# The normalised x tile moves from VectorE to ScalarE at the head of a step, its statistics one tile ahead, and the attention bias is loaded early

## The chip, the cores and the metric

The kernel runs on one core of a Trainium2 chip. The metric is the device time of one execution in microseconds (us). Three executions of the kernel before took 1130.46, 1130.94 and 1133.43 us, with a median of 1130.94 us. TensorE (PE) does the matrix products, VectorE (DVE) and ScalarE (ACT) the work on vectors and the copies out of PSUM, GpSimd (POOL) small work in SBUF, and SyncE (SP) issues nearly all DMAs.

## The reference

One gated cross-attention layer of a Flamingo model, all in f32. x has the shape (4, 2048, 512), the context (4, 77, 384); there are 16 heads of 64, and the feed-forward part is one matrix that is picked out of eight.

```python
def _layernorm(x, axis=-1, eps=1e-05):
    m = jnp.mean(x, axis=axis, keepdims=True)
    v = jnp.var(x, axis=axis, keepdims=True)
    return (x - m) / jnp.sqrt(v + eps)
...
    q = split_heads(x @ Wq)
    k = split_heads(context @ Wk)
    v = split_heads(context @ Wv)
    sim = jnp.einsum('bhid,bhjd->bhij', q, k) * SCALE
    attn = jax.nn.softmax(sim, axis=-1)
    out = jnp.einsum('bhij,bhjd->bhid', attn, v)
    out = out.transpose(0, 2, 1, 3).reshape(b, sq, HEADS * DIM_HEAD)
    return out @ Wo + bo
...
    gumbel = -jnp.log(-jnp.log(u))
    idx = jnp.argmax(jax.nn.log_softmax(logits) + gumbel)
    out = jnp.einsum('btd,de->bte', x, W[idx]) + b[idx]
...
    x = x + jnp.tanh(g_xattn[0]) * _L0_xattn_ref(_layernorm(x), ctx_768, Wq, Wk, Wv, Wo, bo)
    x = x + jnp.tanh(g_ffn[0]) * _L0_ffn_ref(_layernorm(x), W, b, logits, u)
```

## The kernel before, in words

**Folding.** Before the tiles are touched, the query and key weights are folded with the context into one matrix of 512 x (16 x 77) for each of the four batches (`a_split`), and the value and output weights with it into a second one (`vw`, `vw_side`). After that a tile of 128 rows of x needs only this: normalise x (`xn`), multiply by `a_split` (the scores), take the softmax over 77 keys for each head, multiply by `vw` (this is the attention with Wo and bo in it), add to x, normalise again, multiply by the picked feed-forward matrix, add to x.

**Two halves of every number.** Every operand of the large products is f32 split into two f16 halves, a high and a low one, and three products are added up. So each operand passes over ACT (the high half: `x_high`, `probs_high`, `group_high`) and then over DVE (the low half, `low` at L412: `x_low`, `probs_low`, `group_low`), and is then turned (transposed) by a DMA from SP.

**Tiles and steps.** There are 64 tiles. A step `(o, m)` works on tile number 8o+m and on its neighbours; 66 steps run, the first 6 and the last ones unrolled, the others as 7 rounds of a loop of 8 steps (`steps`, L324 to L332). `tile(o, m, lag)` is the tile `lag` steps ahead (o1, m1: the next tile; o2, m2: two tiles back). Every engine has its own `step` with its own hand-written order, and semaphores tie them together.

**The order on each engine in one step of the kernel before**, for tile m:
- PE: the three banks of scores of tile m (`scores`, L1443, 36 products), two products of the feed-forward pair, the attention of tile m-1 (`attention`, L1461), further products of the pair (two in an even step, one in an odd one). The seven products of a pair of tiles are spread over two steps. All pass the helper at L1288. The scores wait for `xT_turned`, the attention for `pT_turned`.
- DVE (L1210): additions of products (`added`, L1191), the moments of x of tile m+1 (L953), the aggregation for tile m-2 (L1147), the largest score of bank 0 (`maxima`, L1111 and L1113), the aggregation for tile m+1 (L957), a low half of a pair group, normalisation of tile m-2 (L1158), bank 1, **the normalisation of x of tile m+1 (`x_normalized`, L964)**, bank 2, additions, **`x_low`**, the softmax factors (L1120, L1122), the low halves of the probabilities, and the sum for the attention of tile m-1 (L1140, L1143).
- ACT (L879): a high half of a pair group (L840), the exponentials of banks 0 and 1 (L817, one instruction a head), **`x_high` (L731) of tile m+1**, another group, the exponentials of bank 2, the high halves of the probabilities (L832, L834, L905).
- POOL (L670): variance to 1/sqrt for tile m-2 (L676, L678) and for tile m+1 (`x_scale`, L601, L603), sums for the pair groups (L692 to L699), the bias (L703).
- SP (L487): in an even step it stores two finished tiles (L497), then loads two tiles of x (L459, after the stores have landed), turns group 2, turns x of tile m+1 (`turn_x`, L444), turns group 3; in an odd step group 0, x, group 1. Last in a step it turns the probabilities (L551).

**Where things lie.** `xn` lies in the room of the high and low probabilities (`ps_words`), so it can be written only when the probabilities of the tile before have been turned. There is one place for the turned x (`xT`), so it is turned only when the scores of tile m are done.

**The prologue.** SP loads context, value weights, two small inputs, output weights, key weights, the picked matrix, query weights, and then the attention bias `bo` (L436) and the first tile. DVE takes the largest value of the output weights, then waits for `bo` (L986), and only behind this come the parts for the value weights, which end in the scale of the folded values. The list VISITS (L346) orders the folding; some units are split on POOL by way of a staging copy (`staged`, `key_staged`). After it DVE works out five small scales (L1090 to L1103). The feed-forward matrix is brought again, four sums of its quarters are made on POOL (`weights_summed`), and its seven operands are split by ACT in step 1 (`weights_high`) and DVE in step 2 (`weights_low`).

## Time and profile before

| what | value |
|---|---|
| median of three executions | 1130.94 us |
| profiled execution | 1130.8 us |
| its span in the trace | 1129.0 us |
| PE busy | 1054.2 us (93%) |
| DVE busy | 884.6 us (78%) |
| ACT busy | 688.2 us (61%) |
| POOL busy | 350.3 us (31%) |
| DMA engines busy, over the whole | 55.5% |

The span runs from the first to the last instruction; 1.8 us of the profiled execution lie around it. A busy share says how long an engine had an instruction in it; it does not say which engine sets the time. In the rows below `[1.04 <-DMA work<-work]` means that the engine had been idle for 1.04 us before this group, and that a DMA from `work` to `work` (a turn) ended the wait. The core's granted TensorE clock was 0.982 of full speed over the span.

### The profile page before, as it was taken

Reading aid. Unit: us, or ns where it says so; the run is one execution under the profiler, and the core shown is the slowest. Engines: PE = TensorE matmul, PEld = TensorE weight load, DVE = VectorE, ACT = ScalarE, POOL = GpSimd, SP = SyncE. Lnnn points to the kernel's source line nnn. Section 1 sums busy time; section 2 is a strip of 40 time slices with the busy share of each in tenths; the row PEclk is TensorE's granted clock in tenths of the full one; section 3 lists DMA queues with packets and bytes.
Section 4 is the critical chain, followed back from the end, with each engine's and each line's share of the span. In section 5 each row is a group of like instructions: output and inputs, shape, how many; then the busy total and the mean of one; then the engine's idle time right before and its main releaser. Section 6 shows DMA issues by size and latency. Waiting matters only on the chain.

```text
span 1129.0 us, 21540 instructions
## 1 busy us (share of the span) xinstructions
PE 1054.2 (93%) x6109; PEld 592.2 (52%) x6109; DVE 884.6 (78%) x1853; ACT 688.2 (61%) x2645; POOL 350.3 (31%) x504
## 2 busy tenths in 40 slices
PE   7778789999999999899999999999989999899997
PEld 5433435555554555555555555555545555455555
DVE  2757778878888888788878887888878888888883
ACT  3257666566656666566666666666657665666670
POOL 0167233223332233322233332333223333223311
PEclk9799989999999999999999999999999999999999
DMA  8131246666665555666566555556665655655563
GB/s 314 39 57 57 61 94 117 127 121 127 131 118 112 112 120 126 127 131 130 119 124 126 125 117 106 114 128 132 135 121 118 135 123 108 121 116 121 126 118 103
DMA packets 381682, 134.33 MB, mean 119 GB/s; under 512 B 360160, under 2 KB 361236, under 8 KB 381588
## 3 DMA queue, kind: packets, MB, share of 16 engines
q1 hardware_dynamic: 381524, 133.43, 55.5%
q14 instruction: 78, 0.64, 0.2%
q8 instruction: 16, 0.26, 0.1%
q0 software_dynamic: 64, 0.00, 0.0%
HBM read 27.21 MB, written 16.78 MB: 39 GB/s over the span
## 4 chain that ended last, share of the span: by engine, by line
DVE 23%; DMA 17%; issue 17%; ACT 16%; PE 15%; SPq 10%; POOL 1%; DVEq 1%; ACTq 0%
ACT work L817 12%; DMA work<-work 11%; PE banks L1288 10%; DVE work L412 6%; SPq L551 6%; DMA out<-work 4%; DVE work L1122 3%; DVE stats L1111 2%; DVE work L1140 2%; DVE stats L953 2%; DVE stats L1143 2%; ACT work L731 2%; SPq L463 2%; DVE work L1191 1%; DVE cst L1120 1%
## 5 line engine op out<-in xcount | busy, mean ns | idle before, releaser
L817 ACT ACTIVATE work<-banks,red,cst 128x77 f32<-128x77 f32 x1024 | 409.8, 423 | 199.8 <-DVE red L1113 198.8
L1288 PE MATMUL banks<-fold_area,work 128*128 128x462 f16 (+1 forms) x2304 | 417.9, 341 | 40.9 <-DMA work<-work 38.9
L1288 PE MATMUL banks<-vw_area,work 128*128 128x512 f16 x1701 | 378.9, 381 | 5.2 <-issue 5.2
L1288 PEld LDWEIGHTS banks<-fold_area,work 128*128 128x128 f16 x2304 | 223.7, 98 | 227.6 <-DMA work<-work 36.6
L412 DVE SCALAR_TENSOR_TENSOR work<-work 128x256 f16<-128x256 f32 (+3 forms) x444 | 241.9, 586 | 119.8 <-ACT work L731 70.7
L1288 PEld LDWEIGHTS banks<-vw_area,work 128*128 128x128 f16 x1701 | 166.4, 98 | 194.2 <-issue 7.5
L817 ACT ACTIVATION_READ_ACCUMULATOR work<-banks,red,cst 128x1 f32 x1024 | 217.0, 212 | 0.0
L676 POOL TENSOR_TENSOR stats<-stats,cst 128x1 f32<-128x1 f32 x64 | 12.1, 189 | 653.9 <-DVE stats L1147 653.9
L840 ACT ACTIVATE work<-work 128x512 f16<-128x512 f32 x124 | 72.5, 585 | 146.0 <-DMA work<-work 128.8
L1288 PE MATMUL banks<-work 128*128 128x256 f16 x1260 | 157.2, 273 | 0.0
L1288 PEld LDWEIGHTS banks<-work 128*128 128x128 f16 x1260 | 123.0, 98 | 30.1
L1191 DVE SCALAR_TENSOR_TENSOR work<-banks,cst,work 128x256 f32<-128x256 f32 x210 | 97.0, 482 | 28.8 <-issue 18.1
L1111 DVE TENSOR_REDUCE stats<-banks 128x6 f32<-128x462 f32 (+1 forms) x192 | 111.1, 579 | 10.2 <-PE banks L1288 7.6
L1122 DVE TENSOR_TENSOR work<-work,cst 128x924 f32<-128x924 f32 (+1 forms) x128 | 102.4, 800 | 4.4
L832 ACT ACTIVATE work<-work 128x768 f16<-128x768 f32 (+1 forms) x128 | 80.6, 630 | 22.3 <-DVE work L1122 22.3
L703 POOL TENSOR_TENSOR work<-work 128x512 f32<-128x512 f32 x64 | 81.2, 1269 | 7.1 <-DVE work L1158 6.1
L1113 DVE TENSOR_SCALAR red<-stats,cst 128x6 f32<-128x6 f32 (+1 forms) x192 | 69.8, 364 | 6.8
L1140 DVE SCALAR_TENSOR_TENSOR work<-banks,cst,work 128x512 f32<-128x512 f32 x64 | 47.7, 746 | 4.8 <-PE banks L1490 4.7
L1143 DVE BATCH_NORM_STATS2 stats<-work 128x6 f32<-128x512 f32 x64 | 44.5, 695 | 2.2
L731 ACT ACTIVATE work<-work 128x512 f16<-128x512 f32 x64 | 41.7, 652 | 4.9 <-DVE work L964 4.9
L953 DVE BATCH_NORM_STATS2 stats<-work 128x6 f32<-128x512 f32 x64 | 43.7, 683 | 0.1
L603 POOL TENSOR_TENSOR stats<-stats,cst 128x1 f32<-128x1 f32 x64 | 41.5, 648 | 5.0
(122 smaller groups left out, 751.5 us busy)
## 6 DMA issues: line engine op xcount, KB each, us to landing
work<-in_x SPq DMA_DIRECT2D x64, 256.0 KB, 2.8
out<-work SPq DMA_DIRECT2D x64, 256.0 KB, 2.2
work<-work SPq DMA_TRANSPOSE x258, 3.2
fold_area<-in_L_xattn_Wo SPq DMA_DIRECT2D x4, 512.0 KB, 10.1
work<-in_L_ffn_W SPq DMA_DIRECT2D x2, 1024.0 KB, 7.1
fold_area<-in_L_xattn_Wq SPq DMA_DIRECT2D x2, 1024.0 KB, 13.0
fold_area<-in_L_xattn_Wk SPq DMA_DIRECT2D x2, 768.0 KB, 12.2
fold_area<-in_L_xattn_Wv SPq DMA_DIRECT2D x2, 384.0 KB, 7.4
```

The lines of the kernel that those rows point to most:

```text
L412: return nc.vector.scalar_tensor_tensor(out=lo, in0=value, scalar=scale, in1=hi, op0=ALU.mult, op1=ALU.subtract)
L551: sp.dma_start_transpose(turned[:, start:, :], ps[:, start * P:]).then_inc(pT_turned, 16)
L703: nc.gpsimd.tensor_tensor(xr[:, m2, :], xr[:, m2, :], bias, ALU.add).then_inc(x2b_ready, 1)
L817: nc.scalar.activation(probs[:, h * J:(h + 1) * J], s_bank(m, k)[:, (h - h0) * J:(h - h0 + 1) * J], ACT.Exp, bias=nmx[:, h:h + 1], scale=e ...
L832: nc.scalar.activation(by_core(ps[:, h0 * CORE:h1 * CORE]), values[:, :, 0:CORE], ACT.Copy, scale=2.0 ** PROB_BITS).then_inc(p_hi, 1)
L840: nc.scalar.activation(group_stage(g)[:, 0, :], value, ACT.Copy, scale=2.0 ** XN_BITS).then_inc(x2_hi, 1)
L1111: nc.vector.reduce_max(mx[:, h0:h1], by_head(s_bank(m, k)), AX.X).then_inc(mx_ready, 1)
L1113: nc.vector.tensor_scalar(nmx[:, h0:h1], mx[:, h0:h1], nexp_scale, None, ALU.mult).then_inc(nmx_ready, 1)
L1122: nc.vector.tensor_tensor(values, values, factors.unsqueeze(2).to_broadcast([P, h1 - h0, J]), ALU.mult).then_inc(p_ready, 1)
L1140: nc.vector.scalar_tensor_tensor(out=xr[:, m, :], in0=o_ps, scalar=o_scale, in1=xr[:, m, :], op0=ALU.mult, op1=ALU.add).then_inc(x2_ready, 1)
L1191: nc.vector.scalar_tensor_tensor(out=half, in0=part, scalar=f_scale, in1=half, op0=ALU.mult, op1=ALU.add).then_inc(f_added, 1)
L1288: mm = nc.tensor.matmul(ps, lhs(l), rhs(r), start=first and n == 0, stop=last and n == 2, skip_group_check=onto)
```

## The change

`xn` is made by ACT instead of DVE, as x times rstd plus (-mean times rstd), for which POOL makes two more small values. ACT does it first in a step, followed at once by `x_high`. Its place is now the second half of `xs` and the first 256 words of `probs`; the probabilities are rotated so that these words belong to the four heads of bank 2, and the exponentials of bank 2 wait for `x_low`. The moments and the scale of x are made for tile m+2 at the end of step m. DVE's order within a step, SP's order in an even step and POOL's order change with it. In the prologue `bo` is loaded before the output weights, the last two staged key units are no longer staged, the small scales are made at KEY 20, the first tile is normalised earlier, and the work on the feed-forward weights is split over two steps. The idle products at the first attention go from 14 to 22.

```diff
         def xn_place(o, m):
-            if is_tile(o, m, 0, 1, 2):
-                return room_a if m == 2 else room_b
-            return ps_words[:, 0:D]
+            return room_b if is_tile(o, m, 0, 1) else xn_late      # xn_late = at(folds - HD, D)
         def key_staged(v):
-            return v % HP in STAGED_KEYS
+            return v < UNITS - HP and v % HP in STAGED_KEYS
+        def probs_of(h0, h1):
+            first = (h0 * J - BANKS[2][0] * J) % HJ
+            return probs[:, first:first + (h1 - h0) * J]
# SP
+            sp.dma_start(room_b, bo...).then_inc(bo_loaded, 16)        # ahead of wo
-            sp.dma_start(room_b, bo...).then_inc(bo_loaded, 16)        # behind wq
-                    for lag in (2, 3):
-                        ... load_x(ol, ml)                             # ahead of turn_group(2)
+                    for lag in (2, 3):
+                        ... load_x(ol, ml)                             # behind turn_group(2)
# POOL
             def x_scale(q1, b1):
                 pool.wait_ge(x_var, nth(q1, b1) + 1)
                 nc.gpsimd.tensor_tensor(ve1, mv1[:, 1:2], eps, ALU.add).then_inc(ve1_ready, 1)
-                pool.wait_ge(ve1_ready, nth(q1, b1) + 1)
+                nc.gpsimd.tensor_tensor(nmean1, mv1[:, 0:1], neg_one, ALU.mult).then_inc(ve1_ready, 1)
+                pool.wait_ge(ve1_ready, nth(q1, b1, 2) + 2)
                 nc.gpsimd.tensor_tensor(rstd1, ve1, neg_half, ALU.pow).then_inc(x_rstd, 1)
+                pool.wait_ge(x_rstd, nth(q1, b1, 2) + 1)
+                nc.gpsimd.tensor_tensor(nm1, nmean1, rstd1, ALU.mult).then_inc(x_rstd, 1)
# POOL, step: x_scale of tile m+2 last, behind the pair sums and the bias (it was of tile m+1, early)
# ACT
+            def x_normalized(o1, m1):
+                act.wait_ge(x_rstd, nth(o1, m1, 2) + 2)
+                if not is_tile(o1, m1, 0, 1):
+                    act.wait_ge(xT_turned, nth(o1, m1, 16))
+                    act.wait_ge(p_lo, nth(o1, m1, 4) - 4)
+                nc.scalar.activation(xn_place(o1, m1), xr[:, m1, :], ACT.Identity, bias=nm1, scale=rstd1).then_inc(xn_ready, 1)
 # exponentials
+                if k == 2 and valid(o1):
+                    act.wait_ge(x_lo, nth(o1, m1) + 1)
 # step
+                if valid(o1):
+                    x_normalized(o1, m1)
+                    x_high(o1, m1)
                 if grouped:
                     group_high_of(*pair, 2 if m % 2 == 0 else 0)
                 if valid(o):
                     exponentials(o, m, 0)
                     exponentials(o, m, 1)
-                if valid(o1) and not is_tile(o, m, 0):
-                    x_high(o1, m1)
+                if is_tile(o, m, 0):
+                    weights_high(AS_LOADED)          # places 0, 1, 6
                 if is_tile(o, m, 1):
-                    weights_high()
+                    weights_high(AS_SUMMED)          # places 4, 3, 2, 5
# DVE, the order of a step after the change
+                added 6 / added 2, 3;  maxima 0;  group_low 2 or 0;  x2_variance;  maxima 1;  x2_normalized
+                maxima 2;  x_low(m+1);  [weights_low in steps 1 and 2];  added 0, 1 / 4, 5;  softmax 0
+                group_low 3 or 1;  x_moments(m+2);  softmax 1;  x_variance(m+2);  probs_low 0, 1;  attention_sum(m-1)
# PE
-                    keep_running(14)
+                    keep_running(22)
```

## Rows read from the trace of the kernel before

**Rows 1.** The page, busy time of the engines
```profile
PE 1054.2 (93%) x6109; PEld 592.2 (52%) x6109; DVE 884.6 (78%) x1853; ACT 688.2 (61%) x2645; POOL 350.3 (31%) x504
```

**Rows 2.** Waits of PE: us in total, times, longest us
```profile
PE banks L1288 <- DMA work<-work: 38.9, 28, 5.3
```

**Rows 3.** Timeline of PE: start us, us, what; first instructions of scores
```profile
188.12 6.42 PE L1288 MATMUL banks<-fold_area,work 128*128 128x462 f16 x36
...
361.78 6.42 PE L1288 MATMUL banks<-fold_area,work 128*128 128x462 f16 x36
391.40 6.42 PE L1288 MATMUL banks<-fold_area,work 128*128 128x462 f16 x36
...
560.66 6.42 PE L1288 MATMUL banks<-fold_area,work 128*128 128x462 f16 x36
576.35 6.43 PE L1288 MATMUL banks<-fold_area,work 128*128 128x462 f16 x36 [1.04 <-DMA work<-work]
594.32 8.11 PE L1288 MATMUL banks<-fold_area,work 128*128 128x462 f16 x36 [2.65 <-DMA work<-work]
...
1088.92 6.42 PE L1288 MATMUL banks<-fold_area,work 128*128 128x462 f16 x36
```

**Rows 4.** Timeline of ACT, DVE and SP, one step
```profile
566.33 0.42 ACT L817 ACTIVATE work<-banks,red,cst 128x77 f32<-128x77 f32 x1 [4.47 <-DVE red L1113]
571.05 0.66 ACT L731 ACTIVATE work<-work 128x512 f16<-128x512 f32 x1
...
560.62 1.65 DVE L412 SCALAR_TENSOR_TENSOR work<-work 128x768 f16<-128x768 f32 x4 [0.55 <-ACT work L834]
568.90 0.47 DVE L1111 TENSOR_REDUCE stats<-banks 128x4 f32<-128x308 f32 x1
571.75 1.22 DVE L412 SCALAR_TENSOR_TENSOR work<-work 128x512 f16<-128x512 f32 x1 [1.30 <-ACT work L731]
...
573.19 1.23 SPq L449 DMA_TRANSPOSE work<-work  x1
```

**Rows 5.** Busy time in a stretch: PE, PEld, DVE, ACT, POOL, PEclk, DMA
```profile
396.00:528.00 132.00, 127.45 (x739) 71.58 (x737) 108.06 (x233) 85.40 (x350) 39.94 (x59) 1.00 0.60 127
```

**Rows 6.** Groups of DVE and ACT between 188.12 and 1088.92 us, shapes apart
```profile
L964 DVE TENSOR_SCALAR work<-work,stats 128x512 f32<-128x512 f32 x58 | 32.0, 552 | 0.7 <-DMA work<-work 0.7
L412 DVE SCALAR_TENSOR_TENSOR work<-work 128x512 f16<-128x512 f32 x145 | 112.4, 775 | 62.1 <-ACT work L731 62.1
L817 ACT ACTIVATE work<-banks,red,cst 128x77 f32<-128x77 f32 x928 | 371.4, 422 | 180.6 <-DVE red L1113 179.7
```

**Rows 7.** The page, groups of POOL
```profile
L603 POOL TENSOR_TENSOR stats<-stats,cst 128x1 f32<-128x1 f32 x64 | 41.5, 648 | 5.0
```

**Rows 8.** Timeline of DVE behind the loop's end
```profile
581.43 0.48 DVE L1191 SCALAR_TENSOR_TENSOR work<-banks,cst,work 128x256 f32<-128x256 f32 x1 [2.99 <-issue]
```

**Rows 9.** The page, DMA issues: KB each, us from issue to landing
```profile
work<-in_x SPq DMA_DIRECT2D x64, 256.0 KB, 2.8
```

**Rows 10.** Timeline of SP, an even step
```profile
584.38 0.97 SPq L459 DMA_DIRECT2D work<-in_x  x2
```

**Rows 11.** Timeline of DVE and PE, prologue
```profile
31.48 0.69 DVE L987 TENSOR_REDUCE cst<-work 128x1 f32<-128x512 f32 x1 [12.00 <-DMA work<-in_L_xattn_bo]
...
25.20 0.27 PE L1294 MATMUL banks<-work,red 128*128 128x128 f32 x1
36.42 0.48 PE L1294 MATMUL banks<-work,red 128*128 128x128 f32 x1 [10.95 <-DVE red L938]
```

**Rows 12.** Timeline of DVE and PE, later prologue
```profile
81.30 0.55 DVE L964 TENSOR_SCALAR work<-work,stats 128x512 f32<-128x512 f32 x1 [2.91 <-POOL stats L603]
...
111.77 12.68 PE L1288 MATMUL banks<-fold_area,work 128*128 128x462 f16 x72 [1.93 <-POOL fold_area L636]
```

**Rows 13.** Timeline of PE, first steps
```profile
139.69 6.43 PE L1288 MATMUL banks<-fold_area,work 128*128 128x462 f16 x36 [0.67 <-DMA work<-work]
157.65 8.25 PE L1288 MATMUL banks<-fold_area,work 128*128 128x462 f16 x36 [5.27 <-DMA work<-work]
```

More of the change, by code:

```diff
@@ L117, in flamingo_layer @@
         c.at = RING * D
-        xs = c.take(D).bitcast(F16).rearrange("p (s n) -> p s n", s=2)
         xT = c.take(D)
@@ L151, in flamingo_layer @@
         free = x2T_at + KT * D
-        v_stage = [at(free, 2 * D).rearrange("p (e n) -> p e n", e=2), at(x2T_at, 2 * D).rearrange("p (e n) -> p e n", e=2)]
+        v_stage = [at(start, 2 * D).rearrange("p (e n) -> p e n", e=2) for start in (x2T_at, free)]
         side_stage = [at(start, B * HEADS * REST).rearrange("p (b n) -> p b n", b=B) for start in (x2T_at + 2 * D, free)]
@@ L373, in key_staged @@
         def key_staged(v):
-            return v % HP in STAGED_KEYS
+            return v < UNITS - HP and v % HP in STAGED_KEYS
         def key_staged_before(v):
-            return v // HP * len(STAGED_KEYS) + sum(h < v % HP for h in STAGED_KEYS)
+            return sum(key_staged(n) for n in range(v))
         def highs_after(n):
@@ L507, in step @@
                         turn_group(2)
+                    for lag in (2, 3):
+                        ol, ml = tile(o, m, lag)
+                        if valid(ol):
+                            load_x(ol, ml)
                     if valid(o1) and not is_tile(o, m, 0):
@@ L670, in step @@
             def step(o, m):
-                o1, m1 = tile(o, m, 1)
+                on, mn = tile(o, m, 2)
                 o2, m2 = tile(o, m, -2)
@@ L874, in weights_high @@
                 act.wait_ge(scale_f_ready, 1)
-                act.wait_ge(wf_summed, 4)
-                for i, part in enumerate((b11, b21, t2, b12, t1, t4, b22)):
+                act.wait_ge(wf_again, 16)
+                for i in places:
+                    if i == 4:
+                        act.wait_ge(wf_summed, 4)
+                    part = (b11, b21, t2, b12, t1, t4, b22)[i]
                     nc.scalar.activation(wf_split[:, i, 0], part, ACT.Copy, scale=scale_f).then_inc(wf_hi, 1)
@@ L893, in step @@
                     exponentials(o, m, 1)
-                if valid(o1) and not is_tile(o, m, 0):
-                    x_high(o1, m1)
                 if grouped:
@@ L1212, in step @@
                 o1, m1 = tile(o, m, 1)
+                on, mn = tile(o, m, 2)
                 op, mp = tile(o, m, -1)
@@ L1219, in step @@
                 multiplied = valid(begun[0]) and paired(*begun)
-                ahead = valid(o1) and not is_tile(o, m, 0)
-                if valid(o2):
-                    dve.wait_ge(x2_stats, nth(o2, m2) + 1)
                 if even and valid(ended[0]) and paired(*ended):
@@ L1246, in step @@
                 if valid(o):
-                    maxima(o, m, 1)
-                if ahead:
-                    x_normalized(o1, m1)
-                if valid(o):
                     maxima(o, m, 2)
+                if valid(o1):
+                    x_low(o1, m1)
+                if is_tile(o, m, 1):
+                    weights_low(AS_LOADED, 0)
+                if is_tile(o, m, 2):
+                    weights_low(AS_SUMMED, len(AS_LOADED))
                 if multiplied:
@@ L1254, in step @@
                     added(*begun, 1 if even else 5)
-                if ahead:
-                    x_low(o1, m1)
-                if grouped and even:
-                    group_low_of(*pair, 3)
                 if valid(o):
                     softmax(o, m, 0)
-                    softmax(o, m, 1)
-                if grouped and not even:
-                    group_low_of(*pair, 1)
+                if grouped:
+                    group_low_of(*pair, 3 if even else 1)
                 if not even and is_tile(*pair, 2 * PAIRS):
                     lone_low(2 * PAIRS + 1)
+                if valid(on):
+                    x_moments(on, mn)
+                if valid(on):
+                    dve.wait_ge(x_stats, nth(on, mn) + 1)
+                if valid(o):
+                    softmax(o, m, 1)
+                if valid(on):
+                    x_variance()
                 if valid(o):
```

111 lines of the change are left out of this document (52 added, 59 removed).

## The prediction

> **What bounds the kernel now.** I read the page's busy shares first. PE is busy for 93% of the span, DVE for 78%, ACT for 61% [rows 1]. PE is the candidate, and only a cut in what PE waits for can save much. Second, PE's waits: the scores wait for a turned x 28 times, 38.9 us in all [rows 2]. Third, PE's timeline, read from the start of one tile's scores to the next. Where nothing waits, two tiles (an even and an odd step) take PE 29.62 us, 361.78 to 391.40, 14.81 each [rows 3]. From tile 5 (188.12) to tile 63 (1088.92) lie 29 pairs in 900.8 us. At 29.62 us they would take 859.0, so **41.8 us** are lost to waits and what follows them: after 2.65 us of waiting the scores of 594.32 took 8.11 us instead of 6.42 [rows 3]. The trace as a whole gives a granted clock of 0.982, so a part of the loss is TensorE at its lower level of 1.2 GHz behind such a pause.
>
> Fourth, one step on the other engines, to see why x is late. The scores start at 560.66. DVE reads the last bank at 568.90, but x's high half starts on ACT only at 571.05, because it stands in ACT's queue behind twelve exponentials that begin at 566.33. DVE has waited 1.30 us for it, writes the low half from 571.75, SP turns it from 573.19, and PE starts at 576.35, 3.16 us after that issue and 1.04 us late [rows 3, 4]. DVE pays this wait in nearly every step: 62.1 us over 58 steps, 1.07 each, and 0.55 us for each normalisation [rows 6]. Meanwhile ACT sits idle before the exponentials, 4.47 us here and 180.6 us in 58 steps, 3.1 each [rows 4, 6].
>
> Last, the prologue. DVE stands 12.00 us at L987 for the attention bias. PE spreads a first maximum at 25.20 and the second only at 36.42, 10.95 us idle [rows 11].
>
> **Part 1, x at the head of ACT's step.** ACT gets one more instruction of 128x512. The nearest rows are the high half, 0.66 us on ACT, and the same normalisation on DVE, 0.55 [rows 4, 6]; this one reads two values per partition, so I put it between 0.55 and 1.0 us and take 0.7. Together with the high half that is 1.4 us, set where ACT idles for 3.1 us on the average [rows 6]. Cost on the path: nothing. If that cover is gone, it is 1.4 us a step behind which all exponentials queue, then the softmax on DVE.
>
> The rule of the Trainium skill that speaks against this is in "ScalarE: Activation LUTs", Rules for kernel authors: add and multiply belong on VectorE, which is the faster per element. Its section What ACT_TABLE_LOAD costs gives 186 + 0.833 N ns and some 93 ns for each pointer operand, by which an estimate for this instruction is 0.80 us. The rows agree that DVE is the faster (0.55 against 0.66), and by the page alone 64 tiles would lose 16 us; the rule looks at one instruction, and the idle time of ACT makes it cheap here, so it changes nothing in the sum.
>
> DVE loses the 0.55 us and the wait of 1.07, 1.6 us a step, of 108.06 us busy in 132 (some 13.0 a step at 124 us for eight) [rows 5, 6]. Left are some 12.4 us of work, against 14.81 of PE. Two waits are new. The new place makes ACT wait for the low halves of the step before; these end about 562.3, just where ACT's idle stretch of 4.47 us begins [rows 4], so this costs nothing unless DVE falls behind. The exponentials of bank 2 wait for `x_low`; behind them queue ACT's high halves and, on DVE, the second softmax. `x_low` follows bank 2's maximum: 568.90 + 0.47, its negation (put at 0.47 too, as it is smaller), and 0.78 for the low half [rows 4, 6] make 570.6. ACT is through banks 0 and 1 at 571.05, and has a group to do yet. Hidden by 0.4 us and the group; without cover ACT waits out the difference.
>
> The turn of x then starts near 570.7 instead of 573.19, 2.5 us earlier, and with the same 3.16 us it lands at 573.9, where PE comes free at 575.3 (576.35 - 1.04) [rows 3, 4]. So the usual wait goes with 1.4 us to spare, and DVE starts its next step earlier besides. What is late next? The turned probabilities. They leave at the end of DVE's step and are used only behind the next scores (6.4 us) and two products; I expect no wait.
>
> **Part 2, the statistics one tile ahead.** POOL gets two more operations on 128x1, at most 0.65 us each [rows 7], and is busy for 31% [rows 1]. The chain now has from the end of one step to the head of the next; three dependent operations make under 2 us (3 x 0.65), while DVE still writes the low halves (1.65 us and its wait of 0.55 [rows 4]). Nothing on the path. The tile loaded in an even step is now read by DVE in the same step. SP issues the loads at 584.38 today, 3.0 us behind DVE's first addition at 581.43; moved behind a turn of 1.23 us they go out near 585.5 and land 2.8 us later, at 588.3 and 588.8 [rows 4, 8 to 10]. DVE reaches these moments behind twelve exponentials, 4.72 us (566.33 to 571.05), that begin some 2 us into its step, and behind the first softmax; that makes 589 or later. Nothing, with little to spare. For its price without them, see the last rival.
>
> **Part 3, the loop's end.** At each of the 7 ends DVE stands still for about 3 us with no one to wait for (2.99 in the row) [rows 8]; the wait and slow scores at 594.32 follow from it. The change does not touch this. The Trainium skill, "Runtime: NRT & Kernel Launch", Instruction fetch mechanics, says that a taken branch out of the fetched window stops the sequencer until its page is there, which agrees with the row. DVE would be 3 us late, and so is x: undisturbed DVE is to issue the turn 8 to 10 us behind the start of scores, with 3 us more 11 to 13, and it lands 3.16 later, at 14.2 to 16.2 against 14.81. I take 3 us as left over in all seven, nearer to the lower end because DVE also starts its step earlier; bounds are 0 and 7 x (2.65 + 1.69) = 30 us [rows 3]. So the steady part gives 41.8 - 3 = **38.8 us**.
>
> **Part 4, the bias early.** Its load goes 3 places up; 256 KB ahead of the output weights delays these by an issue and under 1 us of transfer, and those 12.00 us of waiting nearly vanish. But then DVE meets PE's first spread at 25.20 [rows 11]. Behind it stand a power of two, two parts and the largest, put at 1.9 us together (the row of 128x512 at L987 took 0.69, and they are about as much each or less), so the second spread falls at 27.1 instead of 36.42: **9.3 us**, if loads behind it are in time (the bias itself, last but one, landed at 31.48, and its place is taken by the query weights). Bounds 3 and 12; the nearest row is the 10.95 of PE's idleness.
>
> **Part 5, the later prologue.** The first tile's normalisation leaves DVE, which waited 2.91 us there for POOL. The last staged units leave POOL, for which PE waits 1.93 us before the first scores [rows 12], and come to DVE with two low halves, while the normalisation of tile 1 goes and the small scales move there. I count 2 us from the first and 0.7 from the second: **2.7 us**, bounds 0 and 5.
>
> **Part 6, the first steps.** From the first scores (111.77) to those of tile 2 (139.69) 27.92 us pass [rows 12, 13]. After the change the scores of tile 1 cannot follow at once, as its low half comes behind bank 2 of tile 0: 6.3 (half of 12.68) + 0.47 + 0.47 + 0.78 + 3.16 = 11.2 us after the first. They take 6.4 to 8.1 us, the attention 6.3 (139.69 to 157.65 less the wait of 5.27 and the scores of 6.43), and the 22 idle products, for which no row stands, 2 to 3: 26 to 29 us. I take no change. Then tile 3 waited 5.27 us and its scores took 8.25 instead of 6.43 [rows 13]; this came of DVE and ACT doing seven operands in a row ahead of x. 7.1 us less, of which I give 0.7 back, as DVE has some 13 us of work and latency in a step while PE has 12.7 (6.43 + 6.3) without pair products: **6.4 us**, bounds 2 and 9.
>
> **Sum.** 38.8 + 9.3 + 2.7 + 6.4 = 57.2 us, on a span of 1129.0 that becomes 1071.8; with the 1.8 us around it 1073.6 for an execution. The profiled one (1130.8) stands 0.1 us off the median of 1130.94, so I predict **1074 us**. The tail behind 1088.92 is bound by PE, which no edit shortens there. Highest of all gains: 41.8 + 12 + 5 + 9 = 68, so 1063; lowest: 12 + 3 + 0 + 2 = 17, so 1114.
>
> **Rivals.** (A) *The loop's end stays on the path.* For it speaks that DVE's 3 us come in one piece and that it has 2.4 us a step to make good; against it, that the turn leaves 2.5 us earlier. With 2.65 us left at each of seven ends, and three or four of them slowing the scores by 1.69, 24 us stay instead of 3: 1074 + 21 = 1095 us. (B) *The prologue is bound by its loads or by DVE behind the bias.* DVE had 108.06 of 132 us in the loop and is as dense in the prologue; then the 9.3 us shrink to 3 and part 5 to 0: 1074 + 9 = 1083. (C) *It isn't earlier*: ACT reaches its head late, because its group high halves wait for DMAs, and x's low half still comes at the old time. Then only prologue and first steps gain: 1131 - 18 = 1113. Against it: ACT's 3.1 us of idleness a step. (D) *Slower: the moments wait for their tile.* In every even step DVE, in order, stands at the moments until load and turn have landed, and all behind it (second softmax, low halves, the attention's sum) waits. PE feels it once it has eaten DVE's spare time, 2 x 2.4 us a pair, and with 2.1 us more a pair (41.8 + 18.4 us of gain over 29 pairs) all is lost: from 6.9 us of waiting on the kernel is slower than before. At 8 us it is 1074 + 29 x (8 - 4.8) = 1167. Against it: 2.8 us from issue to landing [rows 9].
>
> **Chances.** Forecast (1064 to 1083) 0.60, A 0.14, B 0.14, C 0.06, D 0.03, no change for any reason 0.03. Range 1063 to 1096 leaves out C, D and the rest. 0.3% is what a measurement can tell here. Faster 0.94, same 0.03, slower 0.03.
>
> **What would show it.** After the change PE's waits for a turn are under 8 us in all, pairs start 29.6 to 30 us apart, also over a loop's end; the turn of x is issued 8 to 10 us behind the start of scores (573.19 - 560.66 = 12.5 before); the second spread is near 27 us; the first scores near 100. Wrong would be: ACT idle ahead of its new instruction for a DMA or POOL; DVE waiting for a load at the moments; scores still at 8 us.

## The result, and the profile after

Four executions of the changed kernel took 1075.98 to 1078.66 us, median 1077.25; of the kernel before, beside it, 1129.03 to 1133.43. The ratio is 0.9525, interval 0.9503 to 0.9548: **53.5 us less, 4.75%**. Predicted were 1074 us and 1063 to 1096. The profiled execution took 1076.78 us, with a span of 1075.0 against 1129.0.

The busy line of the page [rows 1]: PE is the same 1045 to 1054 us busy, now 97% of the span. DVE has lost 35 us, ACT has gained 55 and POOL 81, and none of that is on the path.

```profile
PE 1045.0 (97%) x6117; PEld 593.9 (55%) x6117; DVE 849.8 (79%) x1791; ACT 743.4 (69%) x2709; POOL 431.3 (40%) x629
```

PE's waits [rows 2], in total, times, longest: before, PE waited 28 times for a turned x. Now it waits for one twice (5.8 us, ahead of the scores, `fold_area`) and twice for turned probabilities (4.6 us, ahead of the attention, `vw_area`). All four stand in the first steps; the last wait of the kernel, 3.50 us, is in the tail. The scores of tile 5 begin at 173.36, those of tile 63 at 1032.34, and in between PE waits for nothing.

```profile
PE banks L1308 <- DMA work<-work: 10.3, 4, 4.6
```

PE's timeline (start, duration, what, idle before) for the rows of [rows 3, 11 to 13]: the second spread at 27.35 (36.42 before), the first scores at 96.56 (111.77), the first steps with their four waits, two steady scores a pair (29.62 us) apart, and the tail.

```profile
27.35 0.32 PE L1314 MATMUL banks<-work,red 128*128 128x128 f32 x1 [1.71 <-DVE red L967]
...
96.56 8.10 PE L1308 MATMUL banks<-fold_area,work 128*128 128x462 f16 x36 [2.08 <-issue]
109.26 9.16 PE L1308 MATMUL banks<-fold_area,work 128*128 128x462 f16 x36 [4.59 <-DMA work<-work]
...
140.76 6.43 PE L1308 MATMUL banks<-fold_area,work 128*128 128x462 f16 x36 [1.16 <-DMA work<-work]
151.02 6.00 PE L1308 MATMUL banks<-vw_area,work 128*128 128x512 f16 x27 [3.83 <-DMA work<-work]
...
165.77 6.00 PE L1308 MATMUL banks<-vw_area,work 128*128 128x512 f16 x27 [0.76 <-DMA work<-work]
...
380.70 6.42 PE L1308 MATMUL banks<-fold_area,work 128*128 128x462 f16 x36
...
410.32 6.42 PE L1308 MATMUL banks<-fold_area,work 128*128 128x462 f16 x36
...
1066.57 5.10 PE L1556 MATMUL banks<-work 128*128 128x256 f16 x30 [3.50 <-DMA work<-work]
```

From these rows the 54.0 us of span divide, beside the terms of the prediction:

| stretch | before | after | difference | predicted |
|---|---|---|---|---|
| start to the first scores | 111.77 | 96.56 | -15.2 | -12.0 |
| first scores to those of tile 5 | 76.35 | 76.80 | +0.45 | -6.4 |
| tile 5 to tile 63 | 900.8 | 858.98 | -41.8 | -38.8 |
| tile 63 to the end | 40.1 | 42.7 | +2.6 | 0 |

One steady step [rows 4, 5], timeline of DVE, POOL, ACT and SP, tile scores starting at 558.42:

```profile
557.22 0.81 POOL L608 TENSOR_TENSOR stats<-stats,cst 128x1 f32<-128x1 f32 x1 [4.83 <-DVE stats L986]
558.42 6.42 PE L1308 MATMUL banks<-fold_area,work 128*128 128x462 f16 x36
559.42 0.81 ACT L743 ACTIVATE work<-work,stats 128x512 f32<-128x512 f32 x1 [1.49 <-POOL stats L613]
560.27 0.63 ACT L750 ACTIVATE work<-work 128x512 f16<-128x512 f32 x1
564.87 0.48 DVE L1131 TENSOR_REDUCE stats<-banks 128x4 f32<-128x308 f32 x1 [0.21 <-PE banks L1308]
565.39 0.23 DVE L1133 TENSOR_SCALAR red<-stats,cst 128x4 f32<-128x4 f32 x1
565.52 0.69 DVE L418 SCALAR_TENSOR_TENSOR work<-work 128x512 f16<-128x512 f32 x1
566.45 1.23 SPq L455 DMA_TRANSPOSE work<-work  x1
```

x's high half is ready at 560.90, before the last bank of scores exists. The low half follows the last maximum at once, and the turn of x goes out 8.0 us behind the start of scores (12.5 before). From there it is 6.4 us to the next scores, for a turn that took 3.16 before. DVE, which used to wait for ACT, now waits for PE (91.1 us before its maxima, 1.57 a step). That is what a step bound by PE looks like. Busy time over eight steps (columns as in [rows 5]) gives DVE 98.10 / 8 = 12.3 us a step, and PE all 118.50:

```profile
388.00:506.50 118.50, 118.50 (x690) 67.09 (x689) 98.10 (x213) 85.89 (x329) 49.16 (x73) 1.00 0.61 129
```

### The profile page after: what moved, and what is told of

It reads as the page before. It is cut to its first block, busy times and chain, and to the rows that moved or that the text cites. A ratio compares the mean times of both kernels' runs of the same rounds, so it can differ in the third digit from the quotient of the medians.

```text
span 1075.0 us, 21893 instructions
## 1 busy us (share of the span) xinstructions
PE 1045.0 (97%) x6117; PEld 593.9 (55%) x6117; DVE 849.8 (79%) x1791; ACT 743.4 (69%) x2709; POOL 431.3 (40%) x629
## 4 chain that ended last, share of the span: by engine, by line
PE 90%; DVE 3%; DMA 2%; ACT 2%; POOL 1%; issue 1%; SPq 0%; ACTq 0%
PE banks L1308 82%; PE banks L1510 2%; DMA work<-work 1%; PE banks L1338 1%; PE banks L1347 1%; PE banks L1556 1%; PE banks L1419 1%; ACT work L840 1%; PE banks L1411 1%; DVE vw_area L1042 1%; DMA fold_area<-in_L_xattn_Wv 1%; PE banks L1400 1%; DVE work L418 0%; DVE fold_area L1050 0%; ACT vw_area L793 0%
## 5 line engine op out<-in xcount | busy, mean ns | idle before, releaser
L840 ACT ACTIVATION_READ_ACCUMULATOR work<-banks,red,cst 128x1 f32 x1024 | 224.6, 219 | 0.0
L687 POOL TENSOR_TENSOR stats<-stats,cst 128x1 f32<-128x1 f32 x64 | 12.1, 190 | 294.4 <-DVE stats L1167 294.4
L608 POOL TENSOR_TENSOR stats<-stats,cst 128x1 f32<-128x1 f32 x64 | 50.7, 792 | 186.2 <-DVE stats L986 186.2
L743 ACT ACTIVATE work<-work,stats 128x512 f32<-128x512 f32 x64 | 52.1, 814 | 95.1 <-POOL stats L613 79.4
L1142 DVE TENSOR_TENSOR work<-work,cst 128x924 f32<-128x924 f32 (+1 forms) x128 | 112.7, 880 | 4.4
L1211 DVE SCALAR_TENSOR_TENSOR work<-banks,cst,work 128x256 f32<-128x256 f32 x210 | 94.7, 475 | 21.8 <-issue 18.4
L709 POOL TENSOR_TENSOR work<-work 128x512 f32<-128x512 f32 x64 | 94.5, 1477 | 40.9 <-DVE work L1178 36.8
L863 ACT ACTIVATE work<-work 128x512 f16<-128x512 f32 x124 | 71.8, 579 | 21.8 <-DVE work L1178 17.1
L1133 DVE TENSOR_SCALAR red<-stats,cst 128x6 f32<-128x6 f32 (+1 forms) x192 | 60.1, 313 | 6.8
```

What stands on the lines that cost most here:

```text
L608: nc.gpsimd.tensor_tensor(ve1, mv1[:, 1:2], eps, ALU.add).then_inc(ve1_ready, 1)
L709: nc.gpsimd.tensor_tensor(xr[:, m2, :], xr[:, m2, :], bias, ALU.add).then_inc(x2b_ready, 1)
L743: nc.scalar.activation(xn_place(o1, m1), xr[:, m1, :], ACT.Identity, bias=nm1, scale=rstd1).then_inc(xn_ready, 1)
L840: nc.scalar.activation(probs_of(h, h + 1), s_bank(m, k)[:, (h - h0) * J:(h - h0 + 1) * J], ACT.Exp, bias=nmx[:, h:h + 1], scale=exp_scale, ...
L863: nc.scalar.activation(group_stage(g)[:, 0, :], value, ACT.Copy, scale=2.0 ** XN_BITS).then_inc(x2_hi, 1)
L1133: nc.vector.tensor_scalar(nmx[:, h0:h1], mx[:, h0:h1], nexp_scale, None, ALU.mult).then_inc(nmx_ready, 1)
```

## The experiments

Each kernel ran beside the kernel before on the same chip. Its median there was 1130.8 to 1132.5, so ratios are compared where kernels measured in different groups meet.

### The bias alone

The kernel before, with only this:

```diff
+ sp.dma_start(room_b, bo...).then_inc(bo_loaded, 16)   # ahead of wo
- sp.dma_start(room_b, bo...).then_inc(bo_loaded, 16)   # behind wq
```

> The kernel before with one edit: the attention bias is loaded ahead of the output weights. Theory (as in part 4 of the prediction, with what the changed kernel showed): the second spread on PE falls to about 27.3 us from 36.4, and everything behind keeps the shift, so 9 to 12 us are gained, a time of 1119 to 1122; of the 15.2 us by which the first scores came earlier in the changed kernel the rest (3 to 6 us) belongs to the other edits of the prologue. Rival: the loads or DVE bind behind it and under 5 us are gained (1126 or more).

1121.41 us (1119.65 to 1122.63), ratio 0.9905 [0.9889, 0.9922]: 10.1 us less. PE's timeline:

```profile
26.63 0.32 PE L1294 MATMUL banks<-work,red 128*128 128x128 f32 x1 [1.72 <-DVE red L938]
...
99.53 12.68 PE L1288 MATMUL banks<-fold_area,work 128*128 128x462 f16 x72 [1.93 <-POOL fold_area L636]
```

The second spread moved 9.8 us, the first scores 12.2 (99.53). So one DMA, issued ahead of nine others instead of behind them (the loads of four weights), is worth a fifth of the whole change. The other edits of the prologue brought 3 us by this trace (99.53 to 96.56), but in kernels with the changed prologue the first scores begin anywhere from 93.1 to 97.3, so 2 to 6 us is all that can be said.

### The place in ACT's queue

The changed kernel, with ACT's two instructions behind the exponentials instead of ahead of them. Engine, room and statistics are as changed.

```diff
-                if valid(o1):
-                    x_normalized(o1, m1); x_high(o1, m1)
...
                     exponentials(o, m, 0)
                     exponentials(o, m, 1)
+                if valid(o1):
+                    x_normalized(o1, m1); x_high(o1, m1)
```

> The changed kernel, but ACT normalises x and makes its high half behind the exponentials of banks 0 and 1, where the high half stood before, and not first in a step; all else stays. Theory A (the place in ACT's queue is what freed PE): DVE again waits at the low half, 1 us or more a step, the turn leaves some 2 us later, and PE waits for x again at least at the ends of the loop: 1085 to 1110. Theory B (what freed PE is the work taken off DVE and the statistics a tile ahead, the place in the queue is not needed): DVE's spare time takes the wait and the time stays within 3 us of the changed kernel's 1077.

1147.61 us (1145.41 to 1148.38), ratio 1.0142 [1.0125, 1.0159]. **The change turns from 54 us faster into 16 slower.** Timeline of ACT and DVE, and DVE's waits:

```profile
568.63 0.85 ACT L743 ACTIVATE work<-work,stats 128x512 f32<-128x512 f32 x1
569.51 0.63 ACT L750 ACTIVATE work<-work 128x512 f16<-128x512 f32 x1
570.17 0.86 DVE L418 SCALAR_TENSOR_TENSOR work<-work 128x512 f16<-128x512 f32 x1 [3.31 <-ACT work L750]
571.13 0.42 ACT L840 ACTIVATE work<-banks,red,cst 128x77 f32<-128x77 f32 x1 [0.47 <-DVE work L418]
```
```profile
DVE work L418 <- ACT work L750: 190.5, 63, 8.4
```

ACT is not short of time; its order makes DVE wait 3.0 us a step. I had expected 1085 to 1110. I had counted the lateness of x and left out that the exponentials of bank 2 wait in turn for the low half (the row of 571.13): the two engines wait for each other, one after the other, inside one step. That second wait exists only because the changed kernel keeps `xn` in the room of bank 2's probabilities, so the 70 us or so between the two kernels are the place in the queue and this room together.

### The engine alone

The kernel before, with the normalisation on ACT just ahead of `x_high` in its old place, and the two small values on POOL for it.

```diff
 # ACT, x_high
+                act.wait_ge(x_rstd, nth(o1, m1, 2) + 2)
+                nc.scalar.activation(xn_place(o1, m1), xr[:, m1, :], ACT.Identity, bias=nm1, scale=rstd1)...
 # DVE, step
-                    x_normalized(o1, m1)
```

> The kernel before, but x is normalised by ACT directly in front of its high half, in the old place in ACT's queue and in the old room; POOL makes the two small values; statistics and order as before. Theory A (it is the place in the queue): x is later by ACT's 0.8 us less what DVE's lost 0.55 us gives back, so 0 to 20 us slower, 1131 to 1151. Theory B (it is the offload): DVE's 0.55 us a step come off the path, up to 30 us faster, 1100 to 1115.

1163.65 us (1163.04 to 1164.32), ratio 1.0282 [1.0265, 1.0299]: 32 us slower. DVE's wait for the high half went from 1.07 us a step [rows 6] to 2.5:

```profile
DVE work L412 <- ACT work L741: 160.0, 63, 4.5
```

So taking 0.55 us off DVE is a loss where the 0.8 us that replace it stand on the path. Again I had the sign and too small a size (1131 to 1151 expected).

### The place without the engine

The changed kernel again, for reference, and beside it one in which DVE normalises, as the last thing in the step before; ACT then begins its step with the high half.

```diff
 # DVE, step, last
+                if valid(on):
+                    x_normalized(on, mn)
 # ACT, step, first
-                    x_normalized(o1, m1)          # kept for tile 1
                     x_high(o1, m1)
```

> The changed kernel itself, once more, as the measure for the other runs of this group on the same chip: both theories expect 1075 to 1079 us.

> The changed kernel, but x of tile m+2 is normalised by DVE, last in step m behind the sum for the attention, in the new place; ACT makes only the high half first in a step. Theory A (what matters is that x's high half stands ahead of the exponentials, not which engine normalises): DVE has some 12.3 us of work in 14.81 and takes 0.55 more, so PE still waits for nothing in the loop: within 3 us of the changed kernel. Theory B (the offload from DVE is needed too): DVE's 0.55 us a step and its late end show on PE, 10 to 32 us slower than the changed kernel.

The changed kernel: 1074.52 us (1073.24 to 1076.34), ratio 0.9501 [0.9479, 0.9524]. DVE normalising: 1072.53 (1070.65 to 1076.82), ratio 0.9491 [0.9463, 0.9519]. No difference can be told. In its timeline the high half comes 3.2 us behind the start of scores (554.84), against 1.9 in the changed kernel; the turn of x goes out 8.7 us behind it, and PE waits for it in no steady step:

```profile
557.43 0.53 DVE L994 TENSOR_SCALAR work<-work,stats 128x512 f32<-128x512 f32 x1
558.08 0.63 ACT L750 ACTIVATE work<-work 128x512 f16<-128x512 f32 x1 [2.69 <-DVE work L994]
```

**In the steady part the change buys the place at the head of ACT's step, with its statistics ready; who normalises does not matter.** No run has that place without the statistics a tile ahead, the new room and DVE's new order, so what each of these adds was not measured.

### How much time DVE has to spare

The changed kernel with two, and with four, more `bn_stats` of 128x512 a step on DVE behind the moments, their results unused.

```diff
                     x_moments(on, mn)
+                    for i in range(2):            # and 4
+                        nc.vector.bn_stats(stats[:, 56:62], xr[:, mn, :])...
```

> The changed kernel with two more DVE instructions in every step, moments of the same x tile into unused words, behind the real ones: 1.4 us more of DVE work a step, nothing else. Theory A (DVE has 12.3 us of work, its spare time is 2.5 us a step less the stop of 3 us at a loop's end): 13.7 us still fit in 14.81, PE may wait at the loop's ends for 0 to 2 us each; 1075 to 1090. Theory B (DVE is all but the bound): 1.4 x 58 = up to 80 us slower, 1110 or more.

> The same with four more DVE instructions a step, 2.7 us. Theory A: 12.3 + 2.7 + 0.4 (the stop spread over 8 steps) = 15.4 against 14.81, so DVE becomes the bound and the kernel takes about 0.6 x 58 = 35 us more, 1095 to 1130. Theory B (DVE is all but the bound already): twice the loss of the kernel with two, 1140 to 1235.

With two: 1077.7 us (1074.75 to 1080.06), ratio 0.9531 [0.9508, 0.9554], 3 us above the reference, with overlapping intervals. Over eight steps PE is never idle and DVE is busy for 106.73 of 118.50 us, 90%:

```profile
388.00:506.50 118.50, 118.50 (x689) 66.97 (x688) 106.73 (x229) 85.24 (x329) 49.34 (x73) 1.00 0.61 129
```

With four: 1165.64 (1164.2 to 1167.06), ratio 1.0297 [1.0274, 1.032]. Busy time over 240 us of its loop, then waits of ACT and PE in the whole kernel:

```profile
260.00:500.00 240.00, 221.46 (x1256) 122.05 (x1254) 221.29 (x448) 157.47 (x611) 86.86 (x131) 0.99 0.58 121
```
```profile
ACT work L855 <- DVE work L1142: 220.5, 63, 5.2
...
PE banks L1312 <- DMA work<-work: 54.6, 36, 6.5
```

Eight steps take 131.0 us here (387.13 to 518.17), 16.38 each; DVE is busy for 92% of that, 15.1 us. The work alone, 12.26 + 4 x 0.69 = 15.0, is only 0.2 us over PE's 14.81, yet the step grew by 1.57. DVE's other 1.2 us a step (9.8 us in these eight) are 3.0 us of standing still at the loop's end, 3.1 of waits for the exponentials, the group's high half and POOL, and 3.7 of gaps for which the profile names no wait. The stop and the gaps stand in the changed kernel too, where DVE had time over. I had expected 1095 to 1130 from the work and the stop alone.

How much DVE has to spare lies between the two runs. With two added instructions it still waits for the scores, 4.4 us in eight steps (13.5 in the changed kernel), so its spare time was over 1.4 us a step. With four, 2.8 us, it is gone and PE waits. Why the step then grows by 1.57 us, more than the sum of the work says, is explained only in part.

### The first steps: bias x gate

The first steps were the one term with the wrong sign. Timeline of ACT, DVE and SP in step 2 of the changed kernel:

```profile
134.67 0.72 ACT L912 ACTIVATE work<-work,cst 128x512 f32<-128x512 f32 x1 [5.28 <-DMA work<-in_L_ffn_b]
135.29 0.80 ACT L743 ACTIVATE work<-work,stats 128x512 f32<-128x512 f32 x1
136.13 0.63 ACT L750 ACTIVATE work<-work 128x512 f16<-128x512 f32 x1
136.79 0.69 DVE L418 SCALAR_TENSOR_TENSOR work<-work 128x512 f16<-128x512 f32 x1 [2.67 <-ACT work L750]
137.66 1.24 SPq L455 DMA_TRANSPOSE work<-work  x1
```

An instruction that is run once, the feed-forward bias times its gate, waits for its DMA at the very head of ACT's queue. It stood there before as well. In the trace of the kernel before, ACT waits 3.67 us for the same load in step 2, but DVE is at its seven low halves in a row until 148.2 and has the maximum of bank 1 only at 150.1:

```profile
147.52 0.72 ACT L886 ACTIVATE work<-work,cst 128x512 f32<-128x512 f32 x1 [3.67 <-DMA work<-in_L_ffn_b]
```
```profile
143.56 4.69 DVE L1207 SCALAR_TENSOR_TENSOR work<-work,red 128x512 f16<-128x512 f32 x7
...
149.29 0.79 DVE L1113 TENSOR_SCALAR red<-stats,cst 128x6 f32<-128x6 f32 x1
```

The six exponentials of bank 1 cannot start before that, and x's high half, behind them, came at 152.86. By these rows the load delayed it by some 0.4 us at most. The change splits the seven operands over two steps and puts x ahead of the exponentials; this cover is gone, and the load alone holds x. The experiment moves the instruction:

```diff
-                if is_tile(o, m, 2):
-                    act.wait_ge(bias_loaded, 16); act.wait_ge(gate_ready, 1)
-                    nc.scalar.activation(bias, bias, ACT.Copy, scale=gates[:, 1:2])...
 ...                 # x_normalized, x_high, group, exponentials 0 and 1
+                if is_tile(o, m, 2):
+                    ... the same three lines
```

> The changed kernel with one edit: the multiplication of the feed-forward bias by its gate, which ACT does first in step 2 and for which it waits 5.28 us for a load, comes behind the exponentials of banks 0 and 1 of that step. Theory A (this wait at the head of ACT's step 2 took away the gain of the first steps that was forecast at 6.4 us): x of tile 3 and the softmax of tile 2 come some 4 us earlier, PE's waits of 1.16 and 3.83 us at 140.8 and 151.0 go, and the time falls by 3 to 6 us to 1071 to 1074. Theory B (the first steps are bound by DVE and the slow TensorE clock instead): within 1.5 us of the changed kernel.

1071.94 us (1068.13 to 1073.06), ratio 0.9465 [0.9442, 0.9489]; and once more on another chip, as the control of what follows:

> The control of the two kernels below, the same kernel as the one with bias x gate moved behind the exponentials of banks 0 and 1 in step 2 (no other difference from the changed kernel). It gave 1071.94 us beside 1131.54 for the kernel before. Expected here: 1068 to 1074 us, ratio 0.945 to 0.949. If it comes at 1075 or above, the gain that I put down to the move of bias x gate was scatter of the prologue.

1071.62 us (1069.92 to 1074.96), ratio 0.9474 [0.9448, 0.9501]. PE's wait ahead of tile 3's scores is gone, the one behind them has shrunk from 3.83 to 1.90:

```profile
97.34 6.42 PE L1308 MATMUL banks<-fold_area,work 128*128 128x462 f16 x36 [2.08 <-issue]
108.34 8.71 PE L1308 MATMUL banks<-fold_area,work 128*128 128x462 f16 x36 [4.58 <-DMA work<-work]
...
138.06 6.42 PE L1308 MATMUL banks<-fold_area,work 128*128 128x462 f16 x36
146.38 6.00 PE L1308 MATMUL banks<-vw_area,work 128*128 128x512 f16 x27 [1.90 <-DMA work<-work]
```

From the first scores to tile 5's it is 71.3 us here and 75.3 in the reference run of the changed kernel, both with the first scores at full clock: 4.0 us, in the expected 3 to 6. In the first run of this kernel it is 74.7 us, since its first scores ran at the lower clock (9.28 us). Read from the scores of tile 2 to those of tile 5, which leaves that scatter out, it is 46.4 and 47.3 us in the two traces of the changed kernel and 43.1 in both with the move: 3.3 to 4.2 us. The intervals of the whole times overlap with the reference, so the gain rests on the traces.

### The first steps: the wait for tile 1, and the loads

Two more on top of that. First idle products in PE's wait for the turned x of tile 1; then the loads of tiles 2 and 3 in the prologue as well, with fewer idle products at the first attention.

```diff
 # PE, step, ahead of scores
+                if is_tile(o, m, 1):
+                    all_folded(); keep_running(38)
```
```diff
 # SP, prologue, behind the load of tile 1; left out in step 0
+            sp.dma_start(xr[:, 2, :], x[2, 0:P, :]).then_inc(x_loaded[2], 16)
+            sp.dma_start(xr[:, 3, :], x[3, 0:P, :]).then_inc(x_loaded[3], 16)
 # PE, attention
-                    keep_running(22)
+                    keep_running(8)
```

> As the control, and TensorE fills its wait for the turned x of tile 1 with idle products (38 of the small ones that it already uses elsewhere in the prologue), ahead of the scores of tile 1; nothing of the computation changes. In the changed kernel the scores of tile 1 took 9.16 us after 4.59 us idle, and those of later tiles 6.42. Theory A (TensorE runs slower for a while after it stood idle): the scores of tile 1 take about 6.4 us, and what follows comes 1.7 to 2.7 us earlier: 2 to 2.7 us below the control. Theory B (the next thing that TensorE waits for, the turned probabilities of tile 0, lands when it lands, whatever TensorE does before): the scores are shorter and the wait behind them longer by as much, no difference beyond 0.7 us.

> As the kernel with the filled wait, and x of tiles 2 and 3 is loaded in the prologue right behind tile 1's, where before both were loaded in step 0, and the idle products ahead of the first attention are cut from 22 to 8. In the changed kernel VectorE's moments of tile 2 wait 2.4 us for that load in step 0. Theory A (this wait stands ahead of the first attention's low halves): 1.5 to 2.4 us below the kernel with the filled wait. Theory B: what VectorE waits for next (the exponentials by ScalarE) takes the place of it, no difference beyond 0.7 us; or the two loads push the weights that the folding waits for, and it is slower by up to 2 us.

The filled wait: 1067.78 us (1066.81 to 1069.56), ratio 0.9446 [0.9422, 0.9469], 3.8 below the control. The loads early: **1062.8 us** (1062.59 to 1067.16), ratio **0.9411** [0.9385, 0.9437], a further 5.0 by the medians, with intervals that overlap a little. PE's timelines, of the filled wait first:

```profile
102.85 4.31 PE L1321 MATMUL banks<-work 128*128 128x128 f32 x38
107.59 6.43 PE L1308 MATMUL banks<-fold_area,work 128*128 128x462 f16 x36 [0.43 <-DMA work<-work]
113.86 2.56 PE L1321 MATMUL banks<-work 128*128 128x128 f32 x22
116.26 5.99 PE L1308 MATMUL banks<-vw_area,work 128*128 128x512 f16 x27
```
```profile
94.90 6.42 PE L1310 MATMUL banks<-fold_area,work 128*128 128x462 f16 x36 [2.08 <-issue]
...
105.89 6.43 PE L1310 MATMUL banks<-fold_area,work 128*128 128x462 f16 x36 [0.43 <-DMA work<-work]
112.15 1.04 PE L1323 MATMUL banks<-work 128*128 128x128 f32 x8
113.03 5.99 PE L1310 MATMUL banks<-vw_area,work 128*128 128x512 f16 x27
...
1054.03 3.44 PE L1558 MATMUL banks<-work 128*128 128x256 f16 x30 [3.48 <-DMA work<-work]
```

The granted clock from 105 to 118 us was 0.74 in the control and 1.00 with the wait filled: the 4.58 us of standing still had sent PE to its lower level (1.2 of 2.4 GHz) for a part of the next scores, 8.71 instead of 6.43 us. From first scores to tile 5's it is 71.3, then 68.0, then 65.9 us. Of the first 3.3 us, 2.3 lie between the scores of tile 1 and of tile 2, as expected (2 to 2.7); for the rest I have no cause.

Of the last 5.0 us the steps have only 2.1, again as expected. That kernel differs in two things: the turned probabilities leave 2.5 us earlier behind the first scores, which fits the wait of 2.41 us for them that is gone, and the attention starts 1.5 us earlier behind them, the time of the 14 idle products left out (2.56 to 1.04). No run has one without the other. Another 1.7 is the prologue (96.59 to 94.90), and for that I have no cause but the scatter of the prologue (first scores at 93.1 to 97.3 in kernels that do not differ there). In all these kernels tile 5 to tile 63 takes the same 858.98 us.

### The end: idle products in the wrong place

On top of the fastest:

```diff
 # PE, the last tile's feed-forward product, s = 0 the high half, s = 1 the low
                 for s in range(2):
+                    for _ in range(28 if n == NT - 1 and s == 1 else 0):
+                        nc.tensor.matmul(banks[:, 7, 0:HD], turned[:, 0, 0, 0, :], wf_split[:, 0, 0, 0, :])
                     pe.wait_ge(...)
```

> As the kernel with the loads early, and TensorE fills the last wait of the kernel (3.5 us for the turned low half of the last tile, ahead of the last 30 matmuls) with 28 idle products of 256 columns into a bank that nobody reads; nothing of the computation changes. In the profiles of the kernels with this wait of 3.5 us the last 30 matmuls took 3.44, 4.88, 5.10 and 6.32 us, at a granted clock of 0.69 to 0.88 in that stretch where they were slow. Theory A (the idle stretch lets the clock fall in part of the executions): they take 3.44 us, the runs scatter less than before (1062.6 to 1067.2 us without it), all within 1 us, and the median is 0 to 2 us below that of the kernel with the loads early (1062.8, ratio 0.9411). Theory B (the clock at the end has to do with something else, or the idle products meet the turn's transfer): the scatter stays at 4 us or the wait is longer, and the median is the same or up to 1 us above.

1070.81 us (1066.38 to 1072.46), ratio 0.9472 [0.9459, 0.9486]: **slower than without**. My premise was wrong, as PE's timeline shows:

```profile
1054.78 2.34 PE L1560 MATMUL banks<-work 128*128 128x256 f16 x20 [3.48 <-DMA work<-work]
1056.95 3.22 PE L1552 MATMUL banks<-work 128*128 128x256 f16 x28
1060.01 1.26 PE L1560 MATMUL banks<-work 128*128 128x256 f16 x10
```

The 3.48 us are spent on the high half (ahead of the first 20 of the 30 matmuls), not on the low one. The idle products fell behind the wait, where the low half had long landed, and their 3.22 us went on the path; the profiled span grew by 3.8, of which 0.75 are its prologue's. The ratios are 0.0061 apart, some 7 us, and the 3 us more are not explained by this trace. Nor does the length of the wait decide the clock behind it: the 30 matmuls took 3.44 us after 3.48 us of waiting in the kernel with the loads early, and 4.81 to 5.10 us after only 2.6 in the engine alone and both kernels with added work on DVE. Whether a filled wait would steady the end of the kernel stays open.

## Why the prediction was right, and where not

The total was met closer than its parts. The steady part and the prologue brought 3.0 and 3.2 us more than forecast, the first steps and the tail 6.9 and 2.6 less, and these errors largely cancel; that 1074 and 1077 lie so close is in part luck. The steady part, three quarters of the gain, is not.

- **The steady part (38.8 predicted, 41.8 measured)** went by its mechanism: the turn of x leaves 8.0 us behind the start of scores, nothing is late next, and the experiments show that the place at the head is what it needs and the engine is not. The 3 us that I left over at the loop's ends do not exist, and there are six such stops, not seven (18.4 us in all after the change, 18.1 before): seven rounds are joined by six jumps back. DVE still stands 3.01 us there and ACT 2.53 (timeline at the loop's end), but x has some 3.2 us in hand (6.4 less 3.2). DVE's work before was 12.7 us a step by my own row (108.06 x 124 / 132 / 8), not 13.0, which changes nothing:

```profile
544.98 0.82 ACT L743 ACTIVATE work<-work,stats 128x512 f32<-128x512 f32 x1 [2.53 <-issue]
547.59 0.48 DVE L1211 SCALAR_TENSOR_TENSOR work<-banks,cst,work 128x256 f32<-128x256 f32 x1 [3.01 <-issue]
```

- **ACT's added instruction** takes 0.81 us; I took 0.7, in bounds of 0.55 to 1.0. By the Trainium skill, "ScalarE: Activation LUTs", What ACT_TABLE_LOAD costs, the estimate was 0.80, which this trace bears out. Its Rules for kernel authors prefer VectorE for such work, with a figure for bf16. VectorE is faster here in f32 too (0.53 us), and the time does not depend on it, since ACT idles ahead of it anyway: 74.8 us in 57 steps, waiting for POOL.
- **The statistics ahead** cost nothing, as said. POOL's four small operations take 2.0 us (557.22 to 559.22), and ACT waits for them 1.49 us, as I had listed among the signs of being wrong (ACT idle ahead of its new instruction for POOL). The sign came and meant nothing: the exponentials behind still stand idle for the first maximum in that step, 0.48 us.
- **The prologue (12.0 predicted, 15.2 measured).** The second spread was predicted at 27.1 and came at 27.35. The bias was worth 9.8 us there and 12.2 by the first scores, as the experiment with it alone shows, where I had 9.3. The rest can't be told from the scatter of the first scores.
- **The first steps (6.4 less predicted, 0.45 more measured)** are the step that failed. I laid tile 3's wait of 5.27 us to the seven operands alone, took it away and gave 0.7 back. What I overlooked is the load that the bias x gate waits for at the head of ACT's queue: the seven operands had only covered it. From tile 2 to tile 5 it is 46.4 us instead of 48.4, 2.0 less; with the bias x gate moved it is 43.1, 5.3 less and near the forecast. From the first scores to tile 2, where I took no change, it is 30.4 us instead of 27.9, because the first scores (8.10) and those of tile 1 (9.16) ran at the lower clock. The first of these is scatter between executions: in the second trace of the changed kernel they took 6.41, and the stretch 28.0. PE's waits for a turn are 10.3 us in the first steps and 13.8 with the tail's, where I had said under 8.
- **The tail (0 predicted, +2.6 measured).** PE's wait for the last high half is 3.50 us instead of 2.61, and the 30 matmuls behind it take 5.10 instead of 3.43 at a granted clock of 0.72. The turn of that half was issued 3.51 us before PE started, and 2.62 us before the change. The changed kernel in both its traces and six of the variants show 3.5; the kernel before, the bias alone, the engine alone, DVE normalising and both with added work on DVE show 2.6. I found no reason for it.

**The rivals.** A (the loop's end stays): no, see above. B (the prologue bound by loads): no. C (x no earlier): no; ACT reaches its head late only in step 2. D (the moments wait for their load): it happens once, 2.4 us at tile 2 in step 0, and never in the loop. The early loads took it away.

## What to carry to other kernels

When an engine waits a little in every step, look at what stands in front of its supplier in the supplier's own queue before moving work between engines: with two instructions at the head of ACT's queue the kernel was 4.75% faster than before (most of it from the steady part, a fifth from the bias), and with the same two behind twelve exponentials 1.4% slower. When something is moved to the head of a queue, look for everything that already stands there, also what runs only once, and ask what has hidden it so far. A wait of TensorE can cost twice, once as a wait and once as slow matmuls behind it. Filling the one at tile 1 paid; before filling another, look in the trace which of several waits on one line it is.

## What the runs showed of the hardware

- After 4.6 us idle, PE's 36 matmuls of tile 1 took 8.5 to 9.2 us instead of 6.4 in seven traces of seven, at a granted clock of 0.74 in that stretch in the control; with 38 small products in the wait they took 6.43.
- After the same 2.08 us idle, the first 36 matmuls of the scores took 8.1 to 9.3 us in five traces and 6.4 in six. What decides it stays open.
- DVE at 90% busy over eight steps left PE without a wait; four added instructions of 0.69 us a step, at 92% busy, cost 91 us.
- Six times, a round of the loop apart, DVE stood still for 3.0 to 3.1 us, waiting for nothing that the profile shows.
- The same small turn took 2.6 us from issue to use in some kernels and 3.5 in others (6 and 8 of 14 traces). The reason is open.
